# Two buffers in turn for the turned blocks of the last attention, the second one in memory of the ternary layer

## The chip, the cores and the metric

One core of one Trainium2 chip. The time is the device time of one execution in microseconds (us). Lower is better. A copy of the kernel under a profiler gives the trace.

## What is computed

Two layers on x of shape (4, 256, 256), with a context of shape (4, 256, 128). Layer 0 is a small cross attention and a feed-forward layer with ternary weights. Layer 1 is a cross attention with 16 heads over the context and a feed-forward layer with 8-bit weights. The change touches layer 1's attention only:

```python
q = (text_hidden @ Wq)...; k = (vision_tokens @ Wk)...; v = ...
scores = jnp.einsum('bhtd,bhsd->bhts', q, k) / scale
attn = jax.nn.softmax(scores, axis=-1)
out = jnp.einsum('bhts,bhsd->bhtd', attn, v)
return out @ Wo
...
x = x + _L0_xattn_ref(...); x = x + _L0_ffn_ref(...)
x = x + _L1_xattn_ref(...); x = x + _L1_ffn_ref(...)
```

## The kernel before, in words

The attention of layer 1 is done in 32 steps n (4 batches times 8 pairs of heads). One step works on 512 rows of queries (two heads times 256 rows) against 256 keys. Each engine runs its own list of steps, written out by hand; the lists are fixed orders, and an engine that waits holds up all that stands behind in its list.

In a step, TensorE makes the queries (bank `q`), ScalarE and VectorE split them into a high and a low part (`q_hi`, `q_lo`), TensorE makes the scores, VectorE masks them and takes the row minimum (L1564, `sm`), ScalarE takes the exponential (L981), VectorE inverts the sum (`srec`), and ScalarE and GpSimd normalise two quarters each (`norm_act`, `norm_done`; L999, L662). Matrix products are done as three products of high and low parts, all through the helper at L2016.

The normalised `sm` must be turned (keys to partitions) before TensorE can multiply it by the values. For steps 3 to 29 (27 of 32) this goes in four moves. VectorE turns each 32x32 block into the buffer `blocks` (`turn_blocks`, L1581). SyncE's queue writes the buffer to one half of `block_room` in DRAM with four transfers (`blocks_written`, L442). It reads the half back with two transfers, one for each half c of the keys, into `tp` (`blocks_read`, L455), which has room for two steps. ScalarE copies it to `pT_hi` (L993) and GpSimd takes the difference to `tp_lo` (L667); then TensorE multiplies (`contexts`). ScalarE and VectorE split that result (`oT_hi`, `oT_lo`, L1595), and TensorE makes the output product (`attn_out`).

In what follows, turning k is that of step n = k + 3, so k runs from 0 to 26. There is one `blocks`. `turn_blocks` of turning k waits for `blocks_out` >= 64 k, which says that the writes of turning k - 1 have landed. Between these steps VectorE also does, for the 8-bit weights of the last layer, pairs of small operations on `step8` (`eighths`, L1601 and L1604), sixteen pairs in all.

The ternary layer's rooms lie under one big region (`ffn_room`). `gbuf` (1024 floats in each partition) holds centred rows; `uq` (the same size) holds rounded hidden values until the queue has turned them (`turn_hidden`). The last layer's `fuse`, `f_hi` and `f_lo` use the first 6144 floats of the same region, `gbuf` lies inside them and `uq` behind them.

Of the kernel before, what the change touches and what calls it, by code (L numbers as in the profile page):

```python
# [5 lines left out]
P = 128  # L6
# [17 lines left out]
def xattn_ffn_kernel(nc, x, ctxT, mask, wq0T, bq, wk0T, bk, w_norm, wgvT, woutT, wq, wk, wv, wo,  # L24
# [3 lines left out]
    B, S = mask.shape  # L28
    NT = T // P
    TB = NT // B  # L30
    KD = D // P
    SC = S // P
# [21 lines left out]
    with ExitStack() as ctx:  # L54
        def sem(name):
            return ctx.enter_context(nc.semaphore(name))

        def tile(stack, name, shape, dt=F32):
            return stack.enter_context(nc.sbuf_tensor(name, shape, dt))
# [3 lines left out]
        with ExitStack() as unsplit:  # L63
            tp = tile(unsplit, "tp", [P, 2, SC, 2 * TOK])
# [53 lines left out]
        with ExitStack() as ffn:  # L118
# [3 lines left out]
            gbuf = tile(ffn, "gbuf", [P, 2, TB, D])  # L122
            hqT = tile(ffn, "hqT", [P, 3, KD, TOK], BF16)
            su = tile(ffn, "su", [P, 2, HID])
            uq = tile(ffn, "uq", [P, 2, HID], BF16)
# [48 lines left out]
        sm = tile(ctx, "sm", [P, 2, 4, S])  # L174
        pT_hi = tile(ctx, "pT_hi", [P, SC, 2 * TOK], F32R)

        with ExitStack() as turned:
            blocks = tile(turned, "blocks", [P, S // 32, 4, 32])
# [10 lines left out]
        block_room = nc.dram_tensor("block_room", [2 * S, 2 * TOK], F32).ap()  # L189

        def bank(n):
            return pb[:, n, :]
# [30 lines left out]
        hqT_ps, hqT_done, hq_done = sem("hqT_ps"), sem("hqT_done"), sem("hq_done")  # L223
        hq_turned = sem("hq_turned")
        uq_turned = [sem(f"uq_turned{n}") for n in range(2)]
        y_added, down2_ps = sem("y_added"), sem("down2_ps")
        pT_lo_pool, norm_act = sem("pT_lo_pool"), sem("norm_act")
        blocks_done, blocks_out = sem("blocks_done"), sem("blocks_out")
        blocks_in = [sem(f"blocks_in{c}") for c in range(SC)]
        gate_ps, gate_done, value_ps, silu_done, u_done = (  # L230
            sem("gate_ps"), sem("gate_done"), sem("value_ps"), sem("silu_done"), sem("u_done"))
        umax_done, uqs_done, osc_done, ur_done, uq_done = (
# [60 lines left out]

        SUMS, DOWN = 7, ((5, 6), (2, 7))
        FIRST_TURNED, LAST_TURNED = 3, 29
        GATE_UP_PIECES = -(-2 * KD * INNER // PIECE)
        ctx_raw = xb[:].rearrange("p t d -> p (t d)")[:, NT * D - B * S:]
        CTX = B * S // 2
# [28 lines left out]
        def passing_bank(what, n):  # L327
            return PASSING[place(what, n)][2]
# [11 lines left out]
        def by_blocks(n):  # L340
            return FIRST_TURNED <= n <= LAST_TURNED


        def turns_before(n):
            return min(max(n - FIRST_TURNED, 0), LAST_TURNED - FIRST_TURNED + 1)

        def passed_before(n):
            return n - turns_before(n)
# [12 lines left out]
        def turned_room(n):  # L361
            return turns_before(n) % 2
# [5 lines left out]
        def last_passing(n):  # L368
            return max(k for k, m in enumerate(PASSING) if m[2] == n)

        def turned_queries(i):
            return RAW_HOME[2 + 2 * (i // 2)].rearrange("p (k n) -> p k n", k=KD)[:, :, (i % 2) * 2 * P:(i % 2 + 1) * 2 * P]

        def as_f32(ap):
            return ap.bitcast(F32)
# [5 lines left out]
        def _(sp):  # L381
# [52 lines left out]
            def blocks_written(n):  # L434
                k = turns_before(n)
                sp.wait_ge(blocks_done, k + 1)
                if k >= 2:
                    sp.wait_ge(blocks_in[0], 16 * (k - 1))
                    sp.wait_ge(blocks_in[1], 16 * (k - 1))
                rows = block_room[k % 2 * S:(k % 2 + 1) * S, :].rearrange("(g a) e -> a g e", a=32)  # L440
                for i in range(4):
                    sp.dma_start(rows[:, :, i * P:(i + 1) * P], blocks[32 * i:32 * (i + 1), :, :, :].rearrange("a g k b -> a g (k b)")).then_inc(blocks_out, 16)  # L442

            def blocks_read(n):
                k = turns_before(n)
                if k < 2:
                    sp.wait_ge(base_done, NT // 2 * (k + 1))
                    sp.wait_ge(hq_turned, (16, 48)[k])
                if k >= 2:
                    sp.wait_ge(oT_ps, n - 1)  # L450
                sp.wait_ge(blocks_out, 64 * (k + 1))
                for c in range(SC):
                    if k >= 1:
                        sp.wait_ge(blocks_in[c], 16 * k)
                    sp.dma_start(tp[:, k % 2, c, :], block_room[k % 2 * S + c * P:k % 2 * S + (c + 1) * P, :]).then_inc(blocks_in[c], 16)  # L455

            def eighth(n):
                if n == 0:
# [37 lines left out]
            turn_hidden(2)  # L496
            turn_hidden(3)
            blocks_written(3)
            turn_rows(3)
            blocks_read(3)  # L500
            blocks_written(4)
            blocks_read(4)
            blocks_written(5)
            blocks_read(5)
            blocks_written(6)
            blocks_read(6)
# [355 lines left out]
        def _(act):  # L862
            a = nc.scalar
# [50 lines left out]
            def turned(i):  # L914
                act.wait_ge(turned_ps, 5 + i)
                a.activation(turned_queries(i), bank(passing_bank("turn", i)).rearrange("p (h n) -> p h n", h=2), ACT.Copy).then_inc(turned_done, 1)
# [66 lines left out]

            def probs(n, c):
                if by_blocks(n):
                    act.wait_ge(blocks_in[c], 16 * (turns_before(n) + 1))
                    whole = tp[:, turned_room(n), c, :]
                else:
                    act.wait_ge(pT_ps, SC * passed_before(n) + c + 1)
                    whole = bank(passing_bank("pT", SC * n + c))  # L990
                if n >= 1 and c == 0:
                    act.wait_ge(oT_ps, n)
                a.activation(pT_hi[:, c, :], whole, ACT.Copy).then_inc(pT_hi_done, 1)  # L993
# [17 lines left out]
            def gate4_copy(c):  # L1011
                if c == 0:
                    act.wait_ge(x2_done, NT)
                    act.wait_ge(ld_scales, 48)
                act.wait_ge(g4_ps, c + 1)
                a.activation(fuse[:, c, :], bank(passing_bank("gate4", c)), ACT.Copy).then_inc(g4_done, 1)

# [365 lines left out]
        def _(dve):  # L1383
            v = nc.vector
# [188 lines left out]
            def turn_blocks(n):  # L1573
                k = turns_before(n)
                dve.wait_ge(norm_act, 2 * (n + 1))
                dve.wait_ge(norm_done, 2 * (n + 1))
                if k >= 1:
                    dve.wait_ge(blocks_out, 64 * k)
                elif n >= 1:
                    dve.wait_ge(oT_ps, n)  # L1580
                v.transpose(blocks[:].rearrange("p g k b -> p k g b"), sm[:, n % 2, :, :].rearrange("p k (g b) -> p k g b", b=32)).then_inc(blocks_done, 1)  # L1581

            def probs_low(n, c):
                dve.wait_ge(pT_hi_done, SC * n + c + 1)
                if by_blocks(n):
                    z = turned_room(n)
                    v.tensor_tensor(tp_lo[:, z, c, :], tp[:, z, c, :], as_f32(pT_hi[:, c, :]), ALU.subtract).then_inc(pT_lo_done, 1)
                    return
                if n == LAST_TURNED + 1 and c == 0:
                    dve.wait_ge(blocks_out, 64 * turns_before(n))  # L1590
                v.tensor_tensor(pT_lo[:, c, :], bank(passing_bank("pT", SC * n + c)), as_f32(pT_hi[:, c, :]), ALU.subtract).then_inc(pT_lo_done, 1)  # L1591

            def outputs_low(n):
# [413 lines left out]
        def _(pe):  # L2007
# [13 lines left out]
            def passing(what, n):  # L2021
                k = place(what, n)
                at = PASSING[k][2]
                before = [m for m in range(k) if PASSING[m][2] == at]
                if before:
                    left, count = left_bank(before[-1])
                    pe.wait_ge(left, count)
                return at
# [139 lines left out]
            def turn_queries(i):  # L2168
                raw_landed(2 + 2 * (i // 2))
                at = passing("turn", i)  # L2170
                raw = turned_queries(i)
                for h in range(2):
                    for k in range(KD):
                        last = t_.transpose(bank(at)[:, (2 * h + k) * P:(2 * h + k + 1) * P], raw[:, k, h * P:(h + 1) * P], identf[:])
                last.then_inc(turned_ps, 1)

            def fuse_qk(i):
                pe.wait_ge(turned_done, 5 + i)
                at = passing("qk", i)
                turned = turned_queries(i)  # L2180
                for k in range(KD):
                    for h in range(2):
                        last = t_.matmul(bank(at)[:, (2 * k + h) * P:(2 * k + h + 1) * P], turned[:, h, k * P:(k + 1) * P],
                                         wkvT[:, 0, i, :], start=True, stop=True)
                last.then_inc(fused_qk_ps, 1)
# [97 lines left out]
            def gate4(c):  # L2283
                pe.wait_ge(x4T_lo_done, 2 * (c // KI + 1))
                if c == 0:
                    pe.wait_ge(w8_done, GATE_UP_PIECES)
                at = passing("gate4", c)
# [462 lines left out]
```

## Time and profile before

| | us |
|---|---|
| median of 3 runs | 310.96 |
| lowest and highest run | 310.67 and 313.23 |
| the profiled execution | 312.58 |
| its span from first to last instruction | 310.5 |
| TensorE busy in the span | 293.6 |
| VectorE busy | 260.9 |
| ScalarE busy | 253.7 |
| GpSimd busy | 218.5 |

The profiled execution is 1.6 us longer than the median of the runs; 2.1 us of its time lie outside the span. Matrix instructions overlap in the records, so TensorE's busy time also covers pieces in which little is done. The weight loads ("PEld") run one ahead of the products and show a wait more plainly.

### The profile page before, as it was taken

Reading aid. Unit: us, or ns where it says so; the run is one execution under the profiler, and the core shown is the slowest. Engines: PE = TensorE matmul, PEld = TensorE weight load, DVE = VectorE, ACT = ScalarE, POOL = GpSimd, SP = SyncE. Lnnn points to the kernel's source line nnn. Section 1 sums busy time; section 2 is a strip of 40 time slices with the busy share of each in tenths; the row PEclk is TensorE's granted clock in tenths of the full one; section 3 lists DMA queues with packets and bytes.
Section 4 is the critical chain, followed back from the end, with each engine's and each line's share of the span. In section 5 each row is a group of like instructions: output and inputs, shape, how many; then the busy total and the mean of one; then the engine's idle time right before and its main releaser. Section 6 shows DMA issues by size and latency. Waiting matters only on the chain.

```text
span 310.5 us, 6396 instructions
## 1 busy us (share of the span) xinstructions
PE 293.6 (95%) x1980; PEld 259.9 (84%) x1992; DVE 260.9 (84%) x713; ACT 253.7 (82%) x603; POOL 218.5 (70%) x290
## 2 busy tenths in 40 slices
PE   3968999999999999999999999999999999999994
PEld 2755487798989998979889999999988999899884
DVE  3959999999999999889999986997768897675665
ACT  2398995598999998979999899778899999855460
POOL 3558864556998578999879998886678798952001
PEclk9979999999999999999999999999999999999999
DMA  7996032001326548885878756537645647200103
GB/s 223 367 381 199 35 101 70 1 8 30 93 47 189 157 138 251 220 212 139 228 210 226 199 144 174 161 108 219 182 144 148 179 143 211 68 3 0 36 1 101
DMA packets 54609, 44.59 MB, mean 144 GB/s; under 512 B 11696, under 2 KB 45104, under 8 KB 54576
## 3 DMA queue, kind: packets, MB, share of 16 engines
q1 hardware_dynamic: 54016, 43.93, 49.0%
q10 hardware_dynamic: 560, 0.26, 0.3%
q8 instruction: 16, 0.26, 0.3%
q14 instruction: 17, 0.14, 0.2%
HBM read 27.01 MB, written 15.20 MB: 136 GB/s over the span
## 4 chain that ended last, share of the span: by engine, by line
PE 59%; DVE 20%; DMA 8%; issue 5%; SPq 4%; ACT 2%; DVEq 0%
PE pb L2016 41%; DMA block_room<-blocks 5%; PE pb L2279 5%; PE pb L2314 4%; DMA wraw<-in_wgvT 3%; DVE blocks L1581 3%; SPq L442 2%; DVE sm L1564 2%; PE pb L2130 2%; PE pb L2091 2%; PE pb L2076 2%; DVE wraw L1455 2%; DVE step L1601 1%; PE pb L2227 1%; DVE q_lo L1551 1%
## 5 line engine op out<-in xcount | busy, mean ns | idle before, releaser
L667 POOL TENSOR_TENSOR tp_lo<-tp,pT_hi 128x512 fp32r<-128x512 f32 x54 | 70.0, 1311 | 15.1 <-ACT pT_hi L993 14.8
L981 ACT ACTIVATE sm<-sm,smin 128x256 f32<-128x256 f32 x128 | 63.6, 501 | 4.7 <-DVE smin L1564 4.4
L1564 DVE CUSTOM_DVE_ANT_0 sm<-pb,mask_all 128x256 f32<-128x256 f32 x128 | 47.3, 418 | 5.6 <-PE pb L2016 5.5
L1581 DVE STREAM_TRANSPOSE blocks<-sm 128x1024 f32<-128x1024 f32 x27 | 33.5, 1240 | 7.4 <-DMA block_room<-blocks 7.0
L2016 PE MATMUL pb<-ctx_hi,q_hi 128*128 128x256 f32 x128 | 38.1, 298 | 1.1 <-DVE q_lo L1551 0.6
L662 POOL TENSOR_SCALAR sm<-sm,srec 128x256 f32<-128x256 f32 x64 | 30.5, 488 | 10.4 <-DVE srec L1570 10.4
L2016 PE MATMUL pb<-xT_hi,m_hi 128*128 128x256 f32 x128 | 37.3, 292 | 0.3 <-DVE xT_lo L1540 0.3
L2016 PE MATMUL pb<-n_hi,oT_hi 128*128 128x256 f32 x128 | 37.1, 290 | 0.2 <-DVE oT_lo L1595 0.2
L2016 PE MATMUL pb<-xT_hi,m_lo 128*128 128x256 f32 x128 | 36.2, 283 | 0.0
L2016 PE MATMUL pb<-xT_lo,m_hi 128*128 128x256 f32 x128 | 36.2, 283 | 0.0
L2016 PE MATMUL pb<-ctx_lo,q_hi 128*128 128x256 f32 x128 | 36.2, 282 | 0.0
L2016 PE MATMUL pb<-ctx_hi,q_lo 128*128 128x256 f32 x128 | 36.1, 282 | 0.0
L2016 PE MATMUL pb<-n_hi,oT_lo 128*128 128x256 f32 x128 | 36.1, 282 | 0.0
L2016 PE MATMUL pb<-n_lo,oT_hi 128*128 128x256 f32 x128 | 36.1, 282 | 0.0
L993 ACT ACTIVATE pT_hi<-tp 128x512 fp32r<-128x512 f32 x54 | 31.7, 622 | 2.4 <-PE pb L2016 2.3
L999 ACT ACTIVATE sm<-sm,srec 128x256 f32<-128x256 f32 x64 | 29.0, 504 | 3.3 <-DVE srec L1570 3.3
L583 POOL TENSOR_TENSOR rstd<-ve,nhalf 128x2 f32<-128x2 f32 (+1 forms) x16 | 13.2, 826 | 21.6 <-DVE ve L1413 18.3
L2016 PEld LDWEIGHTS pb<-ctx_hi,q_hi 128*128 128x128 f32 x128 | 24.4, 191 | 3.6 <-DVE q_lo L1551 2.1
L2016 PE MATMUL pb<-pT_hi,cr_hi 128*128 128x512 f32 x64 | 26.5, 415 | 0.5 <-DVE pT_lo L1591 0.5
L2016 PEld LDWEIGHTS pb<-n_hi,oT_hi 128*128 128x128 f32 x128 | 24.4, 191 | 1.7 <-DVE oT_lo L1595 0.6
L2016 PEld LDWEIGHTS pb<-xT_hi,m_hi 128*128 128x128 f32 x128 | 24.5, 191 | 1.5 <-DVE xT_lo L1540 0.5
L2016 PE MATMUL pb<-pT_hi,cr_lo 128*128 128x512 f32 x64 | 25.3, 395 | 0.0
(195 smaller groups left out, 943.0 us busy)
## 6 DMA issues: line engine op xcount, KB each, us to landing
block_room<-blocks SPq DMA_DIRECT2D x108, 128.0 KB, 2.8
tp<-block_room SPq DMA_DIRECT2D x54, 256.0 KB, 3.0
w_raw<-in_w SPq DMA_DIRECT2D x4, 576.0 KB, 4.6
wraw<-in_wgvT SPq DMA_DIRECT2D x4, 512.0 KB, 8.4
wraw<-in_woutT SPq DMA_DIRECT2D x2, 512.0 KB, 9.3
out<-xb SPq DMA_DIRECT2D x4, 256.0 KB, 2.2
xa<-in_x SPq DMA_DIRECT2D x3, 256.0 KB, 4.5
xb<-in_ctxT SPq DMA_DIRECT2D x2, 256.0 KB, 5.1
```

Source lines behind the costliest of these rows:

```text
L442: sp.dma_start(rows[:, :, i * P:(i + 1) * P], blocks[32 * i:32 * (i + 1), :, :, :].rearrange("a g k b -> a g (k b)")).then_inc(blocks_out, 16)
L583: g.tensor_tensor(rstd[:, planes, tiles(b)], ve[:, planes, tiles(b)], nhalf[:, planes, tiles(b)], ALU.pow).then_inc(rstd_done, 1)
L662: g.tensor_scalar(sm[:, n % 2, k, :], sm[:, n % 2, k, :], srec[:, n % 2, k:k + 1], 1.0, ALU.mult, ALU.mult).then_inc(norm_done, 1)
L667: g.tensor_tensor(tp_lo[:, z, c, :], tp[:, z, c, :], as_f32(pT_hi[:, c, :]), ALU.subtract).then_inc(pT_lo_pool, 1)
L981: a.activation(sm[:, n % 2, k, :], sm[:, n % 2, k, :], ACT.Exp, bias=smin[:, n % 2, k:k + 1], scale=-1.0, accum_out=ssum[:, n % 2, k:k + 1 ...
L993: a.activation(pT_hi[:, c, :], whole, ACT.Copy).then_inc(pT_hi_done, 1)
L999: a.activation(sm[:, n % 2, k, :], sm[:, n % 2, k, :], ACT.Identity, scale=srec[:, n % 2, k:k + 1]).then_inc(norm_act, 1)
L1564: v.tensor_tensor_reduce(out=sm[:, n % 2, k, :], in0=bank(passing_bank("s", 2 * n + h))[:, (k % 2) * S:(k % 2 + 1) * S], in1=mask_all[:, b ...
L1581: v.transpose(blocks[:].rearrange("p g k b -> p k g b"), sm[:, n % 2, :, :].rearrange("p k (g b) -> p k g b", b=32)).then_inc(blocks_done, 1)
L2016: last = t_.matmul(dst, a_, b_, start=start and k == 0, stop=stop and k == n - 1, skip_group_check=check)
L2279: last = t_.matmul(dst, weight[:, k, i * P:(i + 1) * P], part[:, k, tok], start=n == 0, stop=n == 2 * KD - 1)
L2314: last = t_.matmul(bank(DOWN[h][n])[:, t * D:(t + 1) * D], part[:, i, rows], down8[:, i, :], start=i == 0 and t == 0 and part is f_hi, sto ...
```

## The change

Turning k with k even goes to `blocks`, as before. With k odd it goes to `gbuf` (k up to 15) or, from k = 17, to `uq`; both are viewed in the layout of `blocks`. The semaphore `blocks_out` becomes two, one for each parity, and a turning waits for the writes of turning k - 2. Turning 1 waits for `hq_done` (GpSimd is done with `gbuf`), and turning 17 for the last transposes out of `uq`. ScalarE's first `gate4_copy`, which writes `fuse` over `gbuf`, waits for the odd writes up to k = 15.

To have a semaphore free, the two semaphores `blocks_in[c]` become one. SyncE now waits for both reads of the step before, ahead of the first read, and ScalarE's copy of half c waits for the reads of both halves.

```diff
-        blocks_done, blocks_out = sem("blocks_done"), sem("blocks_out")
-        blocks_in = [sem(f"blocks_in{c}") for c in range(SC)]
+        blocks_done, blocks_in = sem("blocks_done"), sem("blocks_in")
+        blocks_out = [sem(f"blocks_out{z}") for z in range(2)]
...
+        UQ_TURN = 17
...
+        def turned_blocks(k):
+            if k % 2 == 0:
+                return blocks[:]
+            if k < UQ_TURN:
+                return gbuf[:].rearrange("p z t d -> p (z t d)").rearrange("p (g k b) -> p g k b", k=4, b=32)
+            return as_f32(uq[:].rearrange("p a d -> p (a d)")).rearrange("p (g k b) -> p g k b", k=4, b=32)
...
                 if k >= 2:
-                    sp.wait_ge(blocks_in[0], 16 * (k - 1))
-                    sp.wait_ge(blocks_in[1], 16 * (k - 1))
+                    sp.wait_ge(blocks_in, 16 * SC * (k - 1))
...
-                    sp.dma_start(rows[:, :, i * P:(i + 1) * P], blocks[32 * i:32 * (i + 1), :, :, :].rearrange("a g k b -> a g (k b)")).then_inc(blocks_out, 16)
+                    sp.dma_start(rows[:, :, i * P:(i + 1) * P], turned_blocks(k)[32 * i:32 * (i + 1), :, :, :].rearrange("a g k b -> a g (k b)")).then_inc(blocks_out[k % 2], 16)
...
-                sp.wait_ge(blocks_out, 64 * (k + 1))
+                sp.wait_ge(blocks_out[k % 2], 64 * (k // 2 + 1))
+                if k >= 1:
+                    sp.wait_ge(blocks_in, 16 * SC * k)
                 for c in range(SC):
-                    if k >= 1:
-                        sp.wait_ge(blocks_in[c], 16 * k)
-                    sp.dma_start(tp[:, k % 2, c, :], ...).then_inc(blocks_in[c], 16)
+                    sp.dma_start(tp[:, k % 2, c, :], ...).then_inc(blocks_in, 16)
...
-                    act.wait_ge(blocks_in[c], 16 * (turns_before(n) + 1))
+                    act.wait_ge(blocks_in, 16 * SC * (turns_before(n) + 1))
...
+                    act.wait_ge(blocks_out[1], 64 * (UQ_TURN // 2))
...
-                if k >= 1:
-                    dve.wait_ge(blocks_out, 64 * k)
-                elif n >= 1:
+                if k >= 2:
+                    dve.wait_ge(blocks_out[k % 2], 64 * (k // 2))
+                elif k == 1:
+                    dve.wait_ge(hq_done, B - 1)
+                else:
                     dve.wait_ge(oT_ps, n)
-                v.transpose(blocks[:].rearrange("p g k b -> p k g b"), ...).then_inc(blocks_done, 1)
+                if k == UQ_TURN:
+                    for z in range(2):
+                        dve.wait_ge(uq_turned[z], 16 * (NT // 2 - 1))
+                v.transpose(turned_blocks(k).rearrange("p g k b -> p k g b"), ...).then_inc(blocks_done, 1)
...
-                    dve.wait_ge(blocks_out, 64 * turns_before(n))
+                    dve.wait_ge(blocks_out[0], 64 * ((turns_before(n) + 1) // 2))
```

## Rows read from the trace of the kernel before

**Rows 1.** The windows view, 160 to 210 us: busy time (count) of PE, PEld, DVE, ACT, POOL.

```profile
160.00:210.00 50.00, 49.89 (x369) 46.52 (x369) 44.31 (x138) 43.17 (x116) 43.95 (x57) 1.00 0.60 163
```

**Rows 2.** The page's fourth part: the chain that ended last, by line.

```profile
PE pb L2016 41%; DMA block_room<-blocks 5%; PE pb L2279 5%; PE pb L2314 4%; DMA wraw<-in_wgvT 3%; DVE blocks L1581 3%; SPq L442 2%; DVE sm L1564 2%; PE pb L2130 2%; PE pb L2091 2%; PE pb L2076 2%; DVE wraw L1455 2%; DVE step L1601 1%; PE pb L2227 1%; DVE q_lo L1551 1%
```

**Rows 3.** The waits view, 85 to 270 us: total, times, longest, in us.

```profile
DVE blocks L1581 <- DMA block_room<-blocks: 7.0, 9, 1.9
...
PEld pb L2016 <- DVE q_lo L1551: 2.1, 4, 0.9
...
PEld pb L2016 <- DVE oT_lo L1595: 0.6, 2, 0.4
...
PEld pb L2016 <- DVE xT_lo L1540: 0.5, 1, 0.5
...
PE pb L2016 <- DVE fuse L1629: 0.3, 1, 0.3
```

**Rows 4.** The timeline of VectorE behind turning 3 and around turning 6: start, duration, idle before.

```profile
110.56 0.42 DVE L1564 CUSTOM_DVE_ANT_0 sm<-pb,mask_all 128x256 f32<-128x256 f32 x1 [0.42 <-PE pb L2016]
...
128.37 1.25 DVE L1581 STREAM_TRANSPOSE blocks<-sm 128x1024 f32<-128x1024 f32 x1 [0.88 <-DMA block_room<-blocks]
...
130.11 1.12 DVE L1601 TENSOR_SCALAR step<-w_raw 128x288 int32<-128x288 int32 x1
131.27 1.03 DVE L1604 TENSOR_SCALAR step<-step 128x288 f32<-128x288 f32 x1
```

**Rows 5.** The timeline of GpSimd and of TensorE's weight loads in the same stretch.

```profile
128.52 2.54 POOL L667 TENSOR_TENSOR tp_lo<-tp,pT_hi 128x512 fp32r<-128x512 f32 x2
...
130.24 0.19 PEld L2016 LDWEIGHTS pb<-n_hi,oT_hi 128*128 128x128 f32 x1 [0.37 <-DVE oT_lo L1595]
...
134.23 0.19 PEld L2016 LDWEIGHTS pb<-ctx_hi,q_hi 128*128 128x128 f32 x1 [0.93 <-DVE q_lo L1551]
```

**Rows 6.** The small pairs: all of L1601 (min/median/max ns), and one pair beside GpSimd.

```profile
L1601 DVE TENSOR_SCALAR step<-w_raw x16: 261/489/1472, 86.2 to 263.7; 128x288 int32<-128x288 int32 x16
...
263.73 1.32 DVE L1601 TENSOR_SCALAR step<-w_raw 128x288 int32<-128x288 int32 x1 [0.77 <-POOL w8r L680]
265.09 1.27 DVE L1604 TENSOR_SCALAR step<-step 128x288 f32<-128x288 f32 x1
...
263.60 2.59 POOL L667 TENSOR_TENSOR tp_lo<-tp,pT_hi 128x512 fp32r<-128x512 f32 x2
```

**Rows 7.** The timeline of VectorE: two of the later turnings that waited (16 and 23).

```profile
193.02 1.25 DVE L1581 STREAM_TRANSPOSE blocks<-sm 128x1024 f32<-128x1024 f32 x1 [1.85 <-DMA block_room<-blocks]
...
238.65 1.25 DVE L1581 STREAM_TRANSPOSE blocks<-sm 128x1024 f32<-128x1024 f32 x1 [0.61 <-DMA block_room<-blocks]
```

**Rows 8.** The timeline of TensorE's weight loads after 160 us, where they waited.

```profile
194.90 0.19 PEld L2016 LDWEIGHTS pb<-n_hi,oT_hi 128*128 128x128 f32 x1 [0.24 <-DVE oT_lo L1595]
...
205.29 0.19 PEld L2016 LDWEIGHTS pb<-ctx_hi,q_hi 128*128 128x128 f32 x1 [0.41 <-DVE q_lo L1551]
...
240.64 0.19 PEld L2016 LDWEIGHTS pb<-ctx_hi,q_hi 128*128 128x128 f32 x1 [0.51 <-issue]
```

**Rows 9.** Who used `gbuf`, `uq` and `fuse`: duration min/median/max (ns), first and last start.

```profile
L633 POOL TENSOR_SCALAR xa<-gbuf x3: 617/617/617, 38.1 to 77.9; 128x512 bf16<-128x512 f32 x3
...
L431 SPq DMA_TRANSPOSE uqT<-uq x6: 1232/1280/1602, 76.3 to 185.1; - x6
...
L1016 ACT ACTIVATE fuse<-pb x6: 574/577/589, 221.2 to 271.4; 128x512 f32<-128x512 f32 x6
```

**Rows 10.** The reads of turnings 5 and 17: SyncE, ScalarE and GpSimd timelines.

```profile
128.30 0.82 SPq L455 DMA_DIRECT2D tp<-block_room  x2
...
210.96 3.97 SPq L455 DMA_DIRECT2D tp<-block_room  x4
...
214.59 1.15 ACT L993 ACTIVATE pT_hi<-tp 128x512 fp32r<-128x512 f32 x2
...
215.30 2.56 POOL L667 TENSOR_TENSOR tp_lo<-tp,pT_hi 128x512 fp32r<-128x512 f32 x2 [2.56 <-ACT pT_hi L993]
```

More of the change, by code:

```diff
@@ L450, in blocks_read @@
                     sp.wait_ge(oT_ps, n - 1)
-                sp.wait_ge(blocks_out, 64 * (k + 1))
+                sp.wait_ge(blocks_out[k % 2], 64 * (k // 2 + 1))
+                if k >= 1:
+                    sp.wait_ge(blocks_in, 16 * SC * k)
                 for c in range(SC):
-                    if k >= 1:
-                        sp.wait_ge(blocks_in[c], 16 * k)
-                    sp.dma_start(tp[:, k % 2, c, :], block_room[k % 2 * S + c * P:k % 2 * S + (c + 1) * P, :]).then_inc(blocks_in[c], 16)
+                    sp.dma_start(tp[:, k % 2, c, :], block_room[k % 2 * S + c * P:k % 2 * S + (c + 1) * P, :]).then_inc(blocks_in, 16)
             def eighth(n):
@@ L1576, in turn_blocks @@
                 dve.wait_ge(norm_done, 2 * (n + 1))
-                if k >= 1:
-                    dve.wait_ge(blocks_out, 64 * k)
-                elif n >= 1:
+                if k >= 2:
[3 more added lines that the diff above has]
+                else:
                     dve.wait_ge(oT_ps, n)
-                v.transpose(blocks[:].rearrange("p g k b -> p k g b"), sm[:, n % 2, :, :].rearrange("p k (g b) -> p k g b", b=32)).then_inc(blocks_done, 1)
+                if k == UQ_TURN:
+                    for z in range(2):
+                        dve.wait_ge(uq_turned[z], 16 * (NT // 2 - 1))
+                v.transpose(turned_blocks(k).rearrange("p g k b -> p k g b"), sm[:, n % 2, :, :].rearrange("p k (g b) -> p k g b", b=32)).then_inc(blocks_done, 1)
             def probs_low(n, c):
```

## The prediction

> **What bounds the kernel now.** I read the windows first. From 160 to 210 us TensorE is busy 49.89 of 50 us [rows 1]; the other engines have 6 to 7 us to spare there. So in most of the attention TensorE sets the time, and what VectorE saves is worth only as much as it removes from TensorE's own waits.
>
> Then the chain that ended last [rows 2]. More than half of it is TensorE, but it also runs through the writes of `blocks` (5%) and the turnings (3%), together some 25 us. That looks like a large sum for this change. It is not one: the chain steps to whatever released an instruction last, also where TensorE was being fed all the time in parallel.
>
> Then who waited for whom [rows 3]. Turnings waited for the writes of the turning before 9 times out of 26, 7.0 us in all, 1.9 us at most. That is what the change takes away, in VectorE's time. On TensorE's side the weight loads waited for VectorE in three kinds: 2.1 us for `q_lo`, 0.6 for `oT_lo`, 0.5 for `xT_lo`; one more wait was for a bank that `fuse` frees (0.3 us on the products' row). The sum, 3.5 us, is a ceiling on what a faster VectorE could give this kernel in that stretch: 1.1% of the time, even if every one of those waits were due to the buffer.
>
> **The change, part by part.**
>
> *The nine waits.* I follow each to the next point at which TensorE waited for VectorE.
>
> Turning 3 is one of the short ones. Behind it VectorE sits idle for 0.42 us for TensorE's scores [rows 4], so what it gains is given back at once: 0.
>
> Turning 6 starts 0.88 us late [rows 4]. Behind it stand, in order, an `oT_lo`, a pair on `step8`, another `oT_lo`, a mask and `q_lo`. TensorE waits 0.37 us for the first and 0.93 us for the last [rows 5], 1.3 us in all, so 0.88 us earlier can all be used. What could take it is the pair: its two halves last 1.12 and 1.03 us [rows 4], where the shortest of this kind lasts 0.26 [rows 6]. They end when GpSimd's `tp_lo` pair, which runs from 128.52 to 131.06, and the operation behind it end [rows 5]; VectorE was held by GpSimd. If GpSimd held VectorE to the same instant again, the gain at `q_lo` would be zero. A pair late in the kernel shows what happens when VectorE arrives during the first of two `tp_lo` [rows 6]: it started at 263.73, ended at 265.05, about when the first `tp_lo` of 1.3 us did (263.60 plus 1.3), and its second half ended at 266.36, when the second `tp_lo` did. VectorE gets in between the two. Turning 6 without its wait puts the pair at about 129.2, inside the first `tp_lo` (to 129.8); first half out by 129.9, second by about 131.4 instead of 132.3. So 0.8 us stays. Bounds 0 and 0.9; I take 0.8, by the late pair.
>
> The Trainium skill, page "SBUF — State Buffer", section "Who interferes with whom", states the rule behind this: a `tensor_scalar` of VectorE in a two-port mode and a GpSimd instruction take a shared pair of ports as an exclusive lock, by order of issue, and the loser blocks for the whole instruction. The durations of 0.26 to 1.47 us for one shape [rows 6] agree with it. Where VectorE moves, it decides differently which side blocks; I treat that as a rival below.
>
> From 134 us on, VectorE and TensorE move together: VectorE waits for TensorE's results and TensorE follows, so 0.8 us is carried to the saturated stretch and through it.
>
> Turning 16 waited 1.85 us [rows 7]. VectorE's next step but one is an `oT_lo`, for which TensorE waits 0.24 us at 194.90 [rows 8]; some 12 us later it waits for `q_lo`, 0.41 us at 205.29 [rows 8]. The first goes whole. Of the second I count 0.2: the last load before it feeds a product of 512 columns, so part of 0.41 is no loss. Together 0.45, bounds 0.2 and 0.65. The rest of the 1.85 us falls on a VectorE that TensorE does not wait for.
>
> Turnings 20 to 23 follow one another on VectorE; the last waited 0.61 us [rows 7]. Right behind it come the two `fuse`, and the bank freed by them is what TensorE wants at 240.64, where its loads stop for 0.51 us [rows 8]. 0.61 covers 0.51: gain 0.5, bounds 0.3 (the products' own wait [rows 3]) and 0.5.
>
> Turnings 25 and 26 come where TensorE shows no wait for VectorE. The last turning's data reach it earlier, but it does not stand waiting for them: 0, bound 0.2 above. From 265 us the kernel is TensorE's to the end.
>
> Not touched: the remaining waits for `q_lo` and `xT_lo`, between 150 and 157 us, which come after VectorE had itself been waiting for TensorE.
>
> *The new waits.* Turning 1 waits for GpSimd's use of `gbuf`, which last starts at 77.9 us [rows 9], before the first turning. Turning 17 is the one behind turning 16, at about 198 us; the transposes of `uq` were issued last at 185.1 [rows 9]. ScalarE writes `fuse` first at 221.2 [rows 9]; turning 15 was written before 193.02, since turning 16 waited for it. All zero. Queued behind them would be the whole of VectorE's or ScalarE's list.
>
> *One semaphore for both reads.* This is a cost that the change's main part does not need. ScalarE's copy of the first half now waits for the second half too. The two issues of a step's reads last 0.82 us together [rows 10], so the second half is issued about 0.4 us behind the first. The tightest place is turning 17: the reads are issued from 210.96, and ScalarE starts the copy at 214.59, without having been idle [rows 10]; the row shows no wait for the DMA, and nowhere else in the trace does that copy wait for one. GpSimd does wait 2.56 us for this copy [rows 10], so it is here that a later copy would be passed on. But the reads were late because the write of turning 18 stood ahead of them in SyncE's queue; with VectorE ahead by the 1.85 us of turning 16 they come earlier. Cost 0; bounds 0 and 0.8, both issues once. On SyncE, a first read that waited for its own half of the step before now waits for both, again 0.4 us or somewhat more, where two steps are read back to back (turnings 7 and 8, 17 and 18, 21 and 22). Queued behind it is the next write. ScalarE took these blocks later than they landed; 0.
>
> *The queue.* SyncE's order is unchanged: the write of turning k + 1 still stands behind the read of k (or, in four places, ahead of it), which waits for k's writes to land. So the transfers do not overlap more than before, and the write of k + 1 leaves earlier only by what is left of the turning's 1.25 us after the two issues of the read, some 0.5 us. VectorE is freed, the DMA path hardly.
>
> The sum: 0.8 + 0.45 + 0.5 = 1.75 us, say 1.8. Against the profiled execution: 312.58 becomes 310.8, and the span 310.5 becomes 308.7. The median before stands 1.6 us below that execution; I take the difference as independent of the change: 310.96 - 1.8 = 309.2 us.
>
> **The rivals.**
>
> *Swallowed.* GpSimd's hold on VectorE's pairs, or another of the steps behind a turning, absorbs what is gained; or a saving at 134 us is met by the next wait for GpSimd or ScalarE. For it: at 110.56 exactly this happens [rows 4]. Against it: the two waits at 130 and 134 us lie straight behind a late turning. With the 0.8 gone and half of the rest: 1.8 - 0.8 - 0.5 = 0.5 us, 310.5.
>
> *All of it.* The waits between 115 and 157 us are links of one row of VectorE work, and an earlier start loosens each. TensorE recovers the whole 3.5 us: 307.5. Against it: two of the waits follow idle time of VectorE.
>
> *The full 7 us*, as the chain suggests: 304.0. Against it stands [rows 1]: TensorE has nothing like that to give. I leave it out.
>
> *The pairs fall badly (slower).* Sixteen pairs are done; a pair costs about 0.6 us free (twice the shortest half, and a little) and 2.6 beside a `tp_lo` pair (263.73 to 266.36), 2.0 us more [rows 6]. VectorE's moved position can put a free pair beside one. It decides only if this happens where VectorE is what TensorE waits for, in 110 to 157 us. One such pair costs more than the sum above: +0.2, 311.2; two give -1.8 + 4.0 = +2.2, 313.2. Against it: in that stretch most pairs are held already, and can as well become free.
>
> By the lock rule of the Trainium skill's "SBUF — State Buffer" (same section) this is what an engine that runs ahead does: it takes the port that GpSimd was to have, or loses it.
>
> *It does not do what it says*: had turnings still to wait, for instance for the room in DRAM, nothing would change, 311.0. SyncE's wait for the reads is behind the turning, not before it, so I see no way.
>
> **How the numbers follow.** Forecast 309.2: chance 0.50, its own range 308.6 to 310.0. Swallowed or without effect, 310.0 to 311.2: 0.25. All of it, below 308.6: 0.13. Slower by the pairs or by the one semaphore, above 311.2: 0.12. For 8 in 10 I go from 307.8 (0.07 left below) up to 311.6 (0.08 left above). About 1% is what a measurement of this kernel tells from no change: 3.1 us. Faster by more, below 307.9, is only the end of "all of it": 0.08. Slower by more, above 314.1, needs three bad pairs: 0.03. Within 1%: 0.89.
>
> **What would show it.** In the profile after: turnings never wait for `block_room` writes; VectorE's idle of 7.0 us there is gone, but its idle for TensorE, ScalarE and GpSimd has grown by most of it. The weight loads' waits at 130 and 134, 194.9, 205.3 and 240.6 us are gone or shorter, those between 150 and 157 are not. TensorE's busy time is nearly the same. ScalarE's copy L993 shows no wait for the DMA. The prediction is wrong if that copy waits, if the pairs' summed duration moves by over 2 us, or if TensorE's waits shrink and the span does not.

## The result, and the profile after

| | before | after |
|---|---|---|
| median of 20 runs, us | 312.25 | 310.09 |
| lowest to highest | 310.65 to 313.79 | 308.66 to 311.34 |
| the profiled execution | 312.58 | 310.49 |
| its span | 310.5 | 308.4 |

The change makes the kernel 0.7% faster: ratio 0.9929, 95% interval 0.991 to 0.9947. The prediction was 309.2 from a median of 310.96, which is -0.6%; seventeen more runs moved the median before up by 1.3 us. So the gain, 2.16 us, is near the 1.8 us that were forecast, and the time itself, 310.09, lies 0.9 us above the forecast.

The page after, its first and fourth part:

```profile
PE 292.7 (95%) x1980; PEld 259.8 (84%) x1992; DVE 260.3 (84%) x713; ACT 253.4 (82%) x603; POOL 218.3 (71%) x290
...
PE 74%; DVE 12%; ACT 4%; issue 4%; DMA 3%; SPq 2%; POOL 1%; DVEq 0%; ACTq 0%
```

The work is the same to within 1 us on each engine. The chain has lost its links through `block_room` and through the turnings [rows 2]; TensorE's share of it has grown to 74%. The 50 us from 160 to 210 hold 378 products where they held 369 [rows 1], with TensorE "busy" as before (the two stretches don't cut quite the same work out of the list):

```profile
160.00:210.00 50.00, 49.93 (x378) 47.30 (x378) 44.20 (x140) 42.82 (x118) 45.68 (x59) 1.00 0.65 168
```

Who waited for whom after the change, from 85 to 270 us (total, times, longest):

```profile
DVE sm L1572 <- PE pb L2029: 7.0, 8, 1.2
...
DVE srec L1578 <- ACT sm L988: 4.3, 5, 1.3
...
PEld pb L2029 <- DVE q_lo L1559: 0.8, 2, 0.4
...
PEld pb L2029 <- DVE xT_lo L1548: 0.5, 1, 0.5
```

No turning waits for a write any more; there were 7.0 us [rows 3]. TensorE's loads wait 0.8 us for `q_lo`, not 2.1, and for `oT_lo` not at all. The `xT_lo` wait is the same. VectorE's idle time has moved: it waits 7.0 us for the scores, where it waited 5.0 before, and 4.3 us for ScalarE's exponentials at `srec`, where it waited 2.6.

Around turning 6, the timeline of VectorE, then GpSimd's `tp_lo` pair and TensorE's next wait (start, duration, idle before):

```profile
127.32 1.22 DVE L1594 STREAM_TRANSPOSE blocks<-sm 128x1024 f32<-128x1024 f32 x1
...
129.22 0.70 DVE L1614 TENSOR_SCALAR step<-w_raw 128x288 int32<-128x288 int32 x1
129.96 1.28 DVE L1617 TENSOR_SCALAR step<-step 128x288 f32<-128x288 f32 x1
...
128.44 2.63 POOL L674 TENSOR_TENSOR tp_lo<-tp,pT_hi 128x512 fp32r<-128x512 f32 x2
...
133.18 0.19 PEld L2029 LDWEIGHTS pb<-ctx_hi,q_hi 128*128 128x128 f32 x1 [0.38 <-DVE q_lo L1559]
```

The turning starts 1.05 us earlier than in [rows 4]. The first half of the pair lasts 0.70 us and ends at 129.92, between GpSimd's two `tp_lo`; the second ends at 131.24, not at 132.30. The trace has the two `tp_lo` end at 129.75 and 131.07; each half of the pair ends 0.17 us behind one of them. VectorE got the ports after the first `tp_lo` and again after the second, as an exclusive lock would give them; the rule that the prediction cites from the Trainium skill's page "SBUF — State Buffer", section "Who interferes with whom", agrees with these ends. GpSimd's times in a trace are rough, so 0.17 us isn't to be read closely. TensorE's load of this step starts 1.05 us earlier than in [rows 5], and its wait there has fallen from 0.93 to 0.38 us; the one at 130 us is gone. After 190 us, TensorE's loads show none of the waits of [rows 8].

### The profile page after: what moved, and what is told of

It is laid out like the page before. It is cut to its first block, busy times and chain, and to the rows that moved or that the text cites. A ratio compares the mean times of both kernels' runs of the same rounds, so it can differ in the third digit from the quotient of the medians.

```text
span 308.4 us, 6398 instructions
## 1 busy us (share of the span) xinstructions
PE 292.7 (95%) x1980; PEld 259.8 (84%) x1992; DVE 260.3 (84%) x713; ACT 253.4 (82%) x603; POOL 218.3 (71%) x290
## 4 chain that ended last, share of the span: by engine, by line
PE 74%; DVE 12%; ACT 4%; issue 4%; DMA 3%; SPq 2%; POOL 1%; DVEq 0%; ACTq 0%
PE pb L2029 52%; PE pb L2292 7%; PE pb L2327 4%; DMA wraw<-in_wgvT 3%; PE pb L2104 2%; PE pb L2143 2%; PE pb L2089 2%; DVE wraw L1463 2%; PE pb L2205 1%; DVE sm L1572 1%; PE pb L2240 1%; DVE su L1518 1%; DVE m_lo L1511 1%; ACT su L967 1%; ACT sm L988 1%
## 5 line engine op out<-in xcount | busy, mean ns | idle before, releaser
L1608 DVE TENSOR_TENSOR oT_lo<-pb,oT_hi 128x512 fp32r<-128x512 f32 x32 | 21.6, 679 | 4.2 <-ACT oT_hi L1012 4.1
```

What stands on the lines that cost most here:

```text
L1608: v.tensor_tensor(oT_lo[:, n % 2, :], bank(passing_bank("ctx", n)), as_f32(oT_hi[:, n % 2, :]), ALU.subtract).then_inc(oT_lo_done, 1)
```

## A ruler for the stretches

TensorE takes the steps in a fixed order, so the time from its first product of the scores of one step to that of another tells where a kernel loses time. It is read from TensorE's timeline (`pb<-ctx_hi,q_hi`, the first of each step n). For the kernel before, steps 11 and 12:

```profile
128.48 0.28 PE L2016 MATMUL pb<-ctx_hi,q_hi 128*128 128x256 f32 x1
...
134.23 0.39 PE L2016 MATMUL pb<-ctx_hi,q_hi 128*128 128x256 f32 x1 [0.44 <-DVE q_lo L1551]
```

That is 5.75 us from step 11 to step 12 before; after it is 128.39 to 133.18, 4.79. In this pair of traces three stretches hold nearly all that the nine waits cost: 11 to 12 (turning 6), 21 to 22 (turning 16) and 24 to 28 (turnings 20 to 23). "0 to 31" is nearly the whole attention. For all kernels of this study, one profiled execution each, in us:

```
                    11-12  21-22  24-28   0-31    turnings that wait for the write before
before               5.75   8.33  25.52  193.83   all
a1_one_sem           4.77   8.57  25.21  193.02   all
a2_all_wait          4.78   8.04  26.14  194.24   all
c1_sp_both           4.76   8.52  25.32  193.54   all
c2_act_both          4.79   8.86  26.92  195.51   all
a3_free_6            4.79   8.60  27.50  196.20   all but 6
b2_free_20_23        5.76   9.31  25.02  194.77   all but 20 to 23
b3_held_20_23        4.77   8.04  25.52  192.36   20 to 23
a4_held_6            5.77   8.04  25.02  192.80   6
after                4.79   8.04  25.02  191.81   none
b1_two_in            4.77   8.04  25.02  191.78   none
b4_low_first         4.78   8.04  25.02  191.82   none
d1_one_extra         5.77   9.88  28.28  203.78   all, one write more
d2_two_extra         6.07   8.04  25.02  193.89   none, one write more
```

The trace of before is the mildest of the five kernels marked "all" without the extra write. By the waits view, 85 to 270 us, their turnings waited:

| | times | us in all |
|---|---|---|
| before | 9 | 7.0 |
| a1_one_sem | 12 | 7.6 |
| c2_act_both | 11 | 11.3 |
| a2_all_wait | 15 | 12.4 |
| c1_sp_both | 14 | 12.8 |

So "9 of 26, 7.0 us", from which the prediction worked, was a low draw.

## The experiments

Each kernel was timed in five rounds against the kernel before, on the same chip, and profiled once. The chip was one for a1 to a4, another for b1 to b4 and a third for c1 to d2; a difference of ratios between these groups is less certain than one inside a group.

**a1, the single semaphore alone.** The kernel before, with the reads of a block on one semaphore.

```diff
-        blocks_in = [sem(f"blocks_in{c}") for c in range(SC)]
+        blocks_in = sem("blocks_in")
...
+                if k >= 1:
+                    sp.wait_ge(blocks_in, 16 * SC * k)
                 for c in range(SC):
-                    if k >= 1:
-                        sp.wait_ge(blocks_in[c], 16 * k)
...
-                    act.wait_ge(blocks_in[c], 16 * (turns_before(n) + 1))
+                    act.wait_ge(blocks_in, 16 * SC * (turns_before(n) + 1))
```

> The kernel before with one change: the reads of a block count on one semaphore (SyncE waits for both reads of the step before, ScalarE's copy for both halves). One buffer, all nine waits stay. Theory of the places: this part costs nothing, because the copies start 0.4 us or more behind the second half's landing; span 310.5 +- 0.5 us, ratio to before 1.000 +- 0.002, and ScalarE's copy L993 shows no wait for the DMA. Rival, the merged semaphore is a cost that the second buffer pays back: the span grows by 0.6 us or more. Rival, the gain comes from the merged semaphore: the span falls to about 308.5.

Ratio 1.0058 (1.0021 to 1.0095), a loss of some 1.8 us; the profiled execution, with 309.1 us of span, was the fastest of its twelve. The copy L992 of this kernel shows no wait for the DMA there. So the theory that this part costs nothing fails by the timing, and the trace doesn't show why.

**a2, the old wait added to every turning.** The changed kernel with

```diff
+                if k >= 1 and (True):
+                    dve.wait_ge(blocks_out[(k - 1) % 2], 64 * ((k - 1) // 2 + 1))
```

> The changed kernel (two buffers in turn, one semaphore for the reads) with the old wait added to every turning: it also waits for the writes of the turning right before. Theory of the places: all nine waits are back (about 7 us of VectorE's idle time), TensorE's waits at 130, 134, 195, 205 and 240 us are back, and the time is that of the kernel before, ratio 1.000 +- 0.002, span 310.5 +- 0.5. Rival, the gain comes from where the second buffer lies or from the semaphores: the span stays near 308.4.

Ratio 1.0049 (1.001 to 1.0087), span 310.1. The second room and the second write semaphore bring nothing by themselves: what the change gives comes from the turnings not waiting. Without the wait the same kernel is at 0.9929, so not waiting is worth 1.2%, 3.7 us, in this comparison across two sets of runs. Inside one set, a4 below has the wait at a single turning and is at 0.9932, which gives the same 1.2%. The kernel doesn't come back to 1.000, as was expected, but to where a1 stands.

**a3, only turning 6 free.** As a2, with the condition `k != 6`.

> The changed kernel with the old wait on every turning but the sixth, so that only one of the nine waits (0.88 us) is gone. Theory of the places: TensorE's waits at 130 us (0.37 us) goes and that at 134 us falls from 0.93 to about 0.4; the span is 1.0 us below that of the kernel before, 309.5, ratio 0.997; the waits at 195, 205 and 240 us stay. Rival, all of VectorE's idle time counts alike (2.1 us of span for 7.0 us of waits, 0.3 us for each): 0.88 us gives 0.3 us, span 310.2. Rival, GpSimd's hold on the pair of small operations swallows it: no change at 134 us.

Ratio 1.0059 (1.0027 to 1.0092): freeing turning 6 alone gives nothing that can be measured. In a2's trace there was nothing to gain at this place: 11 to 12 took 4.78 with the wait. The span of the profiled execution was 313.2. The ruler says where: 11 to 12 took 4.79 as expected, but 24 to 28 took 27.50 us, 2 us more than before. VectorE's timeline there, turnings 20 to 23:

```profile
222.06 1.25 DVE L1596 STREAM_TRANSPOSE blocks<-sm 128x1024 f32<-128x1024 f32 x1 [2.05 <-DMA block_room<-uq]
...
228.23 1.25 DVE L1596 STREAM_TRANSPOSE uq<-sm 128x1024 f32<-128x1024 f32 x1 [2.22 <-DMA block_room<-blocks]
...
234.14 1.25 DVE L1596 STREAM_TRANSPOSE blocks<-sm 128x1024 f32<-128x1024 f32 x1 [1.48 <-DMA block_room<-uq]
...
240.70 1.25 DVE L1596 STREAM_TRANSPOSE uq<-sm 128x1024 f32<-128x1024 f32 x1 [1.33 <-DMA block_room<-blocks]
```

The same four turnings, by the same rule, waited 0.35, 1.04, 0.38 and 0.61 us in the trace of before (the last one in [rows 7]). The sum here is 7.08 us against 2.38. The turnings are the same, though the two kernels aren't (rooms and semaphores differ). The traces show where the row begins. The four writes of turning 19, from issue to landing, before and then here:

```profile
DMA to landing us min/median/max: 2.5/2.8/3.2
DMA to landing us min/median/max: 2.8/3.1/4.6
```

The turning itself ended at 215.35 and 215.44, the last of its writes landed at 220.17 and 221.94. From there each turning waits for the landing of the one before and then starts the next write, so the late landing is handed down the row: turnings 20 to 23 start 1.8, 2.2, 2.5 and 2.1 us later than in the trace of before. Why that write landed late the traces don't show; in the trace after the change it took 4.9 us, and no turning waited for it. TensorE waits at the end of the row:

```profile
PE pb L2031 <- DVE fuse L1644: 1.3, 1, 1.3
```

This is the bank wait that was 0.3 us before [rows 3].

**a4, only turning 6 held.** As a2, with `k == 6`.

> The changed kernel with the old wait on the sixth turning alone. Theory of the places: the loss is 1.0 us, span 309.4, ratio to before 0.9965; TensorE waits at 130 and 134 us as before the change, and at 195, 205 and 240 us it doesn't. Rival, all of VectorE's idle time counts alike: the loss is 0.3 us, span 308.7.

Ratio 0.9932 (0.9903 to 0.9961): no loss in the runs. In its profiled execution the wait was there and 11 to 12 took 5.77 us, 0.98 more than after. In four of the seven kernels with the wait at turning 6 the stretch took 4.8 us. So this wait costs 1 us in some executions and nothing in others, as its length falls (see the table under "Turning 6" below); the trace of before was one of the former. What was expected, 0.9965, lies just outside the interval.

**b1, two semaphores for the reads again.** The changed kernel; one semaphore is freed by counting the two steps of the identity matrix on one.

```diff
-        blocks_done, blocks_in = sem("blocks_done"), sem("blocks_in")
+        blocks_done = sem("blocks_done")
+        blocks_in = [sem(f"blocks_in{c}") for c in range(SC)]
...
-            g.memset(identf[:], 0.0).then_inc(ident_zero, 1)
+            g.memset(identf[:], 0.0).then_inc(ident_done, 1)
```

> The changed kernel with two semaphores for the two reads again (one is freed by counting the identity's two steps on one semaphore). Theory now: with one buffer the single semaphore cost some 1.8 us (ratio 1.006 when it was tried alone), because the next write stands behind the reads in SyncE's queue and the next turning waited for that write; with two buffers nothing waits for it, so giving the semaphore back changes little: ratio to before 0.993 +- 0.002, as the changed kernel. Rival, the cost of the single semaphore is still paid: ratio 0.987 to 0.989.

Ratio 0.9912 (0.9882 to 0.9942), median 309.30. The best number of the study, but its interval holds that of the change, and on the ruler it is the changed kernel (191.78 against 191.81). With two buffers the single semaphore costs nothing that shows; the interval leaves room for up to some 0.5%.

**b2, only turnings 20 to 23 free**, and **b3, only these held.** As a2, with `not 20 <= k <= 23` and with `20 <= k <= 23`.

> The changed kernel with the old wait on every turning but 20 to 23. Theory now: these four follow each other through the writes' landings, whose times vary from run to run, so this stretch holds most of the gain: against the kernel with all waits (1.005 of before) this one is 2 to 3 us faster, ratio to before 0.996 to 0.999. In the trace, score step 24 to step 28 takes 25.0 us as in the changed kernel, where the kernel with only turning 6 free took 27.5. Rival, the theory of the prediction (0.5 us here, more at turning 6): ratio 1.003.

> The changed kernel with the old wait on turnings 20 to 23 alone. Theory now: most of the gain is lost, ratio to before 1.000 +- 0.003; score step 24 to step 28 takes 25.5 to 27.5 us instead of 25.0, and VectorE waits for writes of blocks 4 times, 2.5 to 7 us in all. Rival, the theory of the prediction: a loss of 0.5 us, ratio 0.9945.

b2: 0.9982 (0.995 to 1.0015). Against all waits (1.0049, on another chip) these four are worth 0.7%, some 2 us, the larger part of the 1.2%; the two intervals just touch. b3: 0.996 (0.9934 to 0.9986). Held alone they cost 0.3% against the changed kernel, 0.5% against b1 of the same set, so 1 to 1.5 us and not most of the gain; the rival's 0.9945 lies in the interval. The two runs don't add up to one worth of these four, and why is not shown. In b3's trace the four waited 5 us in all, and 24 to 28 lost 0.5 us; but c1, with every turning held, waited 4.8 us there and lost 0.3, so this doesn't come from free turnings ahead of the row.

**b4, another of TensorE's waits removed.** The changed kernel, with VectorE's steps `third_low(2)` and `u_max(6)` exchanged.

```diff
             gated_half(6, 1)
-            u_max(6)
             third_low(2)
+            u_max(6)
```

> The changed kernel with two of VectorE's steps exchanged: the low part of the third batch's rows (third_low) ahead of the maximum u_max of the hidden tile 6 (1.22 us). TensorE waits 0.52 us for the former at 155 us in the changed kernel. Theory: TensorE is what counts here, so this wait goes and the span is 0.5 us shorter, ratio to before 0.9915. Rival, the next wait takes its place: no change, 0.993.

Ratio 0.9931 (0.9901 to 0.9962). TensorE's loads around 155 us, after:

```profile
155.32 0.19 PEld L2029 LDWEIGHTS pb<-xT_hi,m_hi 128*128 128x128 f32 x1 [0.52 <-DVE xT_lo L1548]
158.44 0.19 PEld L2029 LDWEIGHTS pb<-pT_hi,cr_hi 128*128 128x128 f32 x1 [0.20 <-issue]
```

and in this kernel, whose times are some 1.2 us lower throughout:

```profile
157.20 0.19 PEld L2029 LDWEIGHTS pb<-pT_hi,cr_hi 128*128 128x128 f32 x1 [0.77 <-issue]
157.23 0.47 PE L2029 MATMUL pb<-pT_hi,cr_hi 128*128 128x512 f32 x1 [0.60 <-DVE oT_lo L1608]
```

The wait of 0.52 us for `xT_lo` is gone, and the next one has grown from 0.20 to 0.77. It is again a wait for VectorE: the product needs the bank that `oT_lo` empties. The exchange moved `xT_lo` forward and left all of VectorE's work ahead of that `oT_lo` as it was, so `oT_lo` ended at the same distance from the first scores (94.9 us in both). "0 to 31" is the same to 0.01 us. A wait of the bounding engine is gained only if the work that it waits for next comes earlier too; reordering VectorE's steps didn't make VectorE earlier, taking its idle time away did.

**c1 and c2, the two halves of the single semaphore**, each on the kernel before: in c1 SyncE waits for both reads ahead of the first, in c2 ScalarE's copy waits for both.

```diff
+                if k >= 1:
+                    sp.wait_ge(blocks_in[0], 16 * k)
+                    sp.wait_ge(blocks_in[1], 16 * k)
                 for c in range(SC):
-                    if k >= 1:
-                        sp.wait_ge(blocks_in[c], 16 * k)
```

> The kernel before (one buffer, two semaphores for the reads) in which SyncE waits for both reads of the step before, ahead of the first read. This is one half of what the single semaphore does, and alone it was 1.006 of before. Theory: where two steps are read back to back the first read leaves some 0.4 us later and the write behind it too, and with one buffer the next turning waits for that write: this half holds the cost, ratio 1.004 to 1.006. Rival, ScalarE's wait is the cost: ratio 1.000.

```diff
-                    act.wait_ge(blocks_in[c], 16 * (turns_before(n) + 1))
+                    act.wait_ge(blocks_in[0], 16 * (turns_before(n) + 1))
+                    act.wait_ge(blocks_in[1], 16 * (turns_before(n) + 1))
```

> The kernel before in which ScalarE's copy of a half waits for both halves. The other half of the single semaphore. Theory: copies start after both have landed anyway, ratio 1.000 +- 0.002. Rival: in runs in which reads land late, the copy waits and TensorE behind it, ratio 1.004 to 1.006.

c1: 1.0002 (0.9972 to 1.0031). c2: 0.9988 (0.996 to 1.0017). Neither half costs anything measurable, so the 0.6% of a1 stays without a cause. The three kernels of the first set that keep nearly all waits came out at 1.005 to 1.006 on one chip, these two at 1.000 on another; the five "all" kernels overlap on the ruler. The wait at the turnings depends on when writes land, and from these runs I can't tell a true cost of the single semaphore with one buffer from a difference in that.

**d1 and d2, a fifth write for each block.** The first 32 partitions are written once more, to a spare place in DRAM that nobody reads, and the waits count five transfers; d1 is the kernel before, d2 the changed one.

```diff
+                spare = spare_room[k % 2 * S:(k % 2 + 1) * S, :].rearrange("(g a) e -> a g e", a=32)
+                sp.dma_start(spare[:, :, 0:P], blocks[0:32, :, :, :].rearrange("a g k b -> a g (k b)")).then_inc(blocks_out, 16)
```

> The kernel before (one buffer) with a fifth transfer behind the four writes of each block: the first 32 partitions are written once more, to a spare place in DRAM, and the next turning and the reads wait for all five. Theory: the landing of a block's writes comes about 0.5 us later; turnings 20 to 23 are linked by it, so the time grows by 4 x 0.5 = 2 us there and by about 1 us elsewhere, ratio 1.008 to 1.012. VectorE waits for writes for 11 us or more, not 7. Rival, the landings aren't what the time hangs on: ratio below 1.003.

> The changed kernel (two buffers) with the same fifth transfer. Theory: no turning waits for writes, and the reads have some microseconds of room, so the time stays within 0.6 us of the changed kernel: ratio to before 0.993 to 0.995. Rival, the path through the reads becomes the one that counts: 2 us more, ratio 1.000.

d1: 1.0289 (1.0257 to 1.0321), 9 us, three times what I expected. The waits view of d1:

```profile
DVE blocks L1584 <- DMA spare_room<-blocks: 24.1, 19, 2.3
...
PE pb L2019 <- DVE fuse L1632: 2.1, 1, 2.1
```

Nineteen turnings wait, 24.1 us in all, where it was 9 to 15 turnings and 7.0 to 12.8 us in the five kernels above. A part of d1's own trace is TensorE's clock: behind the wait of 2.1 us for `fuse`, in a stretch of 4 us (246 to 250) in which TensorE was busy for 1.9, the granted clock was 0.50 from 250 to 253 us, which no other of these traces shows inside the attention. How much of the 9 us this is, was not measured; this trace is also the slowest of d1's six runs. d2: 1.0063 (1.0031 to 1.0095), 4 us above the changed kernel, which was timed on another chip. So the same write costs 9 us with one buffer and about 4 us with two. d2's trace, the fastest of its twelve runs, shows 2.1 us of loss on the ruler, half of that. The second buffer doesn't take all of it: the reads come later too, and now ScalarE's copy waits for them, which it did nowhere in the trace after the change:

```profile
ACT pT_hi L1003 <- DMA tp<-block_room: 6.2, 10, 1.9
```

The rival of d2 was right in kind and too small. Two buffers relieve VectorE, not the path through DRAM. d2 also has the single semaphore, which makes ScalarE's first copy wait for both reads; d2 with two semaphores was not run, so how the 4 us divide is open.

## Why the prediction was right

**The bound, and the ceiling.** TensorE sets the time, and 7.0 us of VectorE's waits gave about 2 us. The chain through `blocks` (8% of the span) was not a sum to be had: right.

**Turning 6, 0.8 us.** In the traces shown it gave 0.96 us (5.75 to 4.79), in the way described, with the pair getting in between two `tp_lo`. But the cost came in three of seven executions. The wait itself was there in all seven; what decides is whether the first half of the pair still starts before GpSimd's first `tp_lo` ends (us, from the traces):

| | wait at turning 6 | pair starts | first `tp_lo` ends | 11 to 12 |
|---|---|---|---|---|
| b2 | 1.03 | 128.78 | 128.34 | 5.76 |
| before | 0.88 | 130.11 | 129.82 | 5.75 |
| a4 | 0.62 | 128.51 | 128.49 | 5.77 |
| c2 | 0.43 | 128.39 | 128.56 | 4.79 |
| a2 | 0.38 | 128.59 | 128.81 | 4.78 |
| c1 | 0.26 | 127.98 | 128.31 | 4.76 |
| a1 | 0.17 | 128.81 | 129.23 | 4.77 |
| after | none | 129.22 | 129.75 | 4.79 |

Up to 0.43 us the wait costs nothing, and from 0.62 us on it costs 0.96 to 0.98, whatever its length: VectorE gets in between the two `tp_lo` or it doesn't. d2, whose pair came behind the first `tp_lo` (129.06 against 128.79) with no wait at the turning, took 6.07. So the mechanism was right, and the size is all or nothing. The mean over the seven is (0.96 + 0.98 + 0.97) / 7 = 0.4 us, and by a4 it can't be measured in the runs.

**Turning 16, 0.45 us.** Before to after, 21 to 22 fell by 0.29, and step 22 to 23 (199.28 to 205.30 before, 197.96 to 203.84 after) by 0.14: 0.43. Over the seven executions in which this turning kept its wait (a3 and b2 with the five "all"), 21 to 22 lies 0.56 us above 8.04 in the mean, from 0 to 1.27, and 22 to 23 another 0.2 above the 5.89 of after. The term was somewhat small.

**Turnings 20 to 23, 0.5 us, "bounds 0.3 and 0.5".** This term was mis-sized. In the trace pair it was 0.50 (25.52 to 25.02). But the seven executions that kept these waits (the five "all", a3, b3) lie 0.2 to 2.5 us above 25.02, 1.0 in the mean. My bounds came from TensorE's wait in one execution; they should have covered what the waits in a row become when a landing is late.

**The sum, 1.8 us.** In the trace pair 0 to 31 fell by 2.02, and the three places account for 1.9 of it (0.96 + 0.43 + 0.50). The five "all" kernels need 194.03 us for 0 to 31 in the mean, the three with none 191.80: 2.2 us, close to the difference of the medians (312.25 - 310.09 = 2.16). Over these five it is made up otherwise: 0.18 in 11 to 12 where the prediction had 0.8, 0.59 in 21 to 23 where it had 0.45, 0.80 in 24 to 28 where it had 0.5, and 0.65 in steps where it had nothing, above all 12 to 21 and 28 to 31. The bound and the mechanism were right; that the total came out so near is partly luck, because the term taken too large and those taken too small made up for each other. These are single executions of kernels that differ in more than the wait, so the parts are rough.

**The time, 309.2 us.** It stood on a median of three runs that was 1.3 us too low. The measured 310.09 lies just outside the forecast's own range (308.6 to 310.0) and inside the 8 in 10; from the profiled execution the prediction had 310.8 and a span of 308.7, and 310.49 and 308.4 were measured.

**Zero for the new waits and the queue.** Right for turnings 1 and 17 and for ScalarE's `fuse`: none shows. VectorE waited 0.59 us at turning 16 and 0.42 at 17 after the change, for the normalisation to end (GpSimd's last part of it ended at 190.65 and at 196.53; the transposes of `uq` were issued last at 184.1):

```profile
190.74 1.25 DVE L1594 STREAM_TRANSPOSE blocks<-sm 128x1024 f32<-128x1024 f32 x1 [0.59 <-issue]
...
196.62 1.25 DVE L1594 STREAM_TRANSPOSE uq<-sm 128x1024 f32<-128x1024 f32 x1 [0.42 <-issue]
```

**Zero for the single semaphore.** With two buffers b1 shows no cost, and ScalarE's copy doesn't wait in the trace after. In the traces of b3 and b4, with the same semaphore, it waits once, for 0.39 and 0.35 us. With one buffer it is open (a1 against c1 and c2).

**The slower rival.** The pairs did not fall badly: their thirty-two halves last 20.7 us in all after, and 21.7 before, within the 2 us that the prediction allowed.

## What to carry to other kernels

A wait for a DMA's landing in one trace is one draw; the same four turnings waited 2.4 us in one trace and 7.1 in another. Where such a wait decides whether an operation slips between two of another engine's, its cost is all or nothing, as at turning 6. Where such waits follow one another in a row, size them by what a late landing does to the whole row, not by the idle time that one trace shows. To place a small gain, measure between fixed points of the bounding engine's own order in several executions; a kernel that adds a wait back at one place is easily made and brings in no race.

## What the runs showed that I had not expected

The second buffer makes the attention nearly the same in the three traces without waits: 191.78, 191.81 and 191.82 us from step 0 to 31, where the five kernels with all the waits spread from 193.02 to 195.51. The kernel had almost no room at the turnings: one write more for each block cost 9 us with one buffer. And the start of the kernel varies by itself: TensorE's first scores came between 61.91 and 63.77 us in these executions, with the same code ahead of them, which is nearly as much as the whole gain and can hide or feign it in a comparison of two spans. Much of it goes with TensorE's clock: in six of the fourteen traces the granted clock fell to 0.50, the lower of its two levels, for some microseconds between 17 and 25 us (0.50 from 18 to 21 us before, 0.61 after, 1.00 in c1), and five of these six have the latest first scores, 62.97 to 63.77; the other eight lie between 61.91 and 62.50. In the 10 us ahead of that, TensorE was busy for 7.6 us before, 8.5 after and 8.4 in c1, so its activity there doesn't tell these cases apart.
